# Attention with one projection per step in the transposes' banks, a score bank per head, and probabilities scaled on GpSimd

## The reference

```python
q = (h @ wq).reshape(b, s, 32, 64).transpose(0, 2, 1, 3)
k, v = ...                      # 8 heads, each repeated for 4 query heads
scores = jnp.einsum('bhqd,bhkd->bhqk', q, k) / jnp.sqrt(64.)
scores = jnp.where(causal, scores, jnp.finfo(scores.dtype).min)
attn = jax.nn.softmax(scores, axis=-1)
out = jnp.einsum('bhqk,bhkd->bhqd', attn, v)
h = x + out.reshape(b, s, 2048) @ wo
```

## Time and profile before

| | us |
|---|---|
| median of 3 runs | 2073.08 (2064.65 to 2074.55) |
| the profiled execution | 2076.18 |
| its span | 2074.5 |
| TensorE matmuls busy | 1878.1 (91%) |
| VectorE busy | 1062.9 (51%) |
| ScalarE busy | 899.0 (43%) |
| GpSimd busy | 234.4 (11%) |

### The profile page before, as it was taken

The page is one execution under the profiler, slowest core; times in us unless marked ns, Lnnn a source line. Parts: engine busy times, 40 slices in busy tenths (PEclk is TensorE's granted clock), DMA queues, the critical chain, the costliest instruction groups (busy, mean ns, idle before and its releaser), DMA issues.

```text
span 2074.5 us, 32988 instructions
## 1 busy us (share of the span) xinstructions
PE 1878.1 (91%) x12734; PEld 1440.2 (69%) x12734; DVE 1062.9 (51%) x1977; ACT 899.0 (43%) x2028; POOL 234.4 (11%) x369
## 2 busy tenths in 40 slices
PE   6999699999999999999999999999934999999970
PEld 5666366766766766766766767767734999999970
DVE  4666466666666666666666666666630111111116
ACT  3444255555555555555555555555530122212210
POOL 2222100000000000000000000000023000000014
PEclk9999799999999999999999999999966999999995
DMA  2000210000000000000000000000025042012503
GB/s 77 0 0 0 100 41 8 1 1 8 1 1 9 1 1 9 1 1 9 1 1 9 1 1 1 1 1 1 1 89 188 26 144 83 25 53 67 196 30 109
DMA packets 44296, 67.25 MB, mean 32 GB/s; under 512 B 9952, under 2 KB 34528, under 8 KB 44192
## 3 DMA queue, kind: packets, MB, share of 16 engines
q1 hardware_dynamic: 35920, 45.11, 6.6%
q0 software_dynamic: 6208, 18.62, 2.7%
q10 hardware_dynamic: 2064, 2.10, 0.3%
HBM read 140.52 MB, written 16.52 MB: 76 GB/s over the span
## 4 chain that ended last, share of the span: by engine, by line
PE 71%; DVE 13%; ACT 7%; issue 5%; POOL 1%; DMA 1%; SPq 1%; DVEq 0%; another core or an unknown queue 0%; POOLq 0%; ACTq 0%
PE wide L1288 13%; PE bank L1208 13%; PE bank L1196 10%; PE wide L1176 7%; PE bank L1297 7%; PE wide L1180 6%; PE bank L1217 3%; ACT qhl L578 3%; DVE qhl L813 3%; PE wide L1152 3%; ACT arena L584 2%; DVE nmax L820 2%; PE wide L1026 2%; PE bank L1015 2%; PE wide L1179 1%
## 5 line engine op out<-in xcount | busy, mean ns | idle before, releaser
L820 DVE TENSOR_REDUCE nmax<-wide 128x1 f32<-128x896 f32 (+7 forms) x512 | 386.6, 755 | 217.5 <-PE wide L1180 207.2
L584 ACT ACTIVATE arena<-wide,nmax 128x896 f32<-128x896 f32 (+7 forms) x512 | 380.6, 744 | 265.4 <-DVE nmax L820 260.4
L1176 PE MATMUL wide<-khi,qhl 128*128 128x512 f32 (+3 forms) x768 | 351.7, 458 | 28.5 <-DVE vt L804 25.1
L1196 PE MATMUL bank<-ident,arena 128*128 128x128 f32 x2304 | 308.5, 273 | 0.0
L592 ACT COPY arena<-bank 128x512 f32<-128x512 f32 (+1 forms) x352 | 192.8, 548 | 253.4 <-PE bank L1196 241.5
L1180 PE MATMUL wide<-klo,qhl 128*128 128x512 f32 (+3 forms) x768 | 300.6, 396 | 0.0
L1208 PE MATMUL bank<-arena,vt 128*64 128x256 f32 x2304 | 295.2, 403 | 0.0
L1288 PEld LDWEIGHTS wide<-wo,arena 128*128 128x128 f32 x2496 | 287.1, 193 | 3.2 <-issue 1.3
L1288 PE MATMUL wide<-wo,arena 128*128 128x128 f32 x2496 | 287.5, 276 | 0.9 <-ACT wo L638 0.9
L1196 PEld LDWEIGHTS bank<-ident,arena 128*128 128x128 f32 x2304 | 261.8, 140 | 8.7 <-issue 0.4
L950 DVE TENSOR_TENSOR wo<-wide,wo 128x512 f32<-128x512 f32 x78 | 54.0, 692 | 415.1 <-PE wide L1288 415.1
(11 more groups left out here) (194 smaller groups left out, 1867.6 us busy)
## 6 DMA issues: line engine op xcount, KB each, us to landing
arena<-in_L_ffn_w SPq DMA_DIRECT2D x117, 1024.0 KB
wo<-xs SPq DMA_DIRECT2D x40, 128.0 KB, 2.0
xs<-zeros POOLq DMA_DIRECT2D x1, 4992.0 KB, 20.6
ys<-y_sb POOLq DMA_DIRECT2D x39, 128.0 KB, 2.0
x_all<-in_L_attn_x ACTq DMA_DIRECT2D x1, 2048.0 KB, 9.9
wq_g<-in_L_ffn_wq SPq DMA_DIRECT2D x8, 256.0 KB, 2.9
wo<-in_L_ffn_wo SPq DMA_DIRECT2D x16, 128.0 KB, 8.0
out<-x_all SPq DMA_DIRECT2D x16, 128.0 KB
```

The costliest lines, as they stand in the source:

```text
L584: nc.scalar.activation(probs[t % 2][:, h, 0:w], score_bank(h)[:, 0:w], ACT.Exp, bias=nmax[:, t % 2, h:h + 1], accum_out=rsum[:, t % 2, h:h ...
L820: nc.vector.tensor_reduce(nmax[:, t % 2, h:h + 1], score_bank(h)[:, 0:w], AX.X, ALU.max, negate=True).then_inc(S("nmax_ready"), 1)
L1176: mm(dst, q, khi[:, lo:lo + cols], start=True, stop=False)
L1196: ins = nc.tensor.transpose(turned[j % 3][:, h * P:(h + 1) * P], probs[t % 2][:, h, m * P:(m + 1) * P], ident[:])
```

## The change

- Each step projects at most one item, at its end (`STEP_ITEM`, in the order H0, H1, H2, V2, F0, F1, F2, V1), and the item takes its turn in the three banks of the transposes (`TURNS`, `bank_of`, `wait_bank`). The first half of V is projected a step before its sequence.
- In tiles 0 to 3 of a sequence each head's scores have a bank of their own. In tiles 4 to 7 the pairs stay. The waits of score(t, h) follow from it (`scores_read`), and the fifth tile doesn't wait for items.
- The reciprocals are no longer spread or transposed. VectorE inverts the sums of two heads at a time (`invert`). GpSimd multiplies the probabilities in place, one head at a time (`normalise`): heads 0 and 1 in the step of the tile, heads 2 and 3 in the next. A tile's first transpose waits for all four.
- The product into `oT` becomes a copy on ScalarE, after exponent(t, 0).

```diff
-PLACES = {(0, "a"): "V1", (0, "b"): "H0", (1, "a"): "H1", (1, "b"): "H2", (2, "a"): "F0", (2, "b"): "F1", (3, "a"): "F2", (3, "b"): "V2"}
...
+STEP_ITEM = ["H0", "H1", "H2", "V2", "F0", "F1", "F2", "V1"]
...
+    kind, i = STEP_ITEM[ct]
+    if kind == "H":
+        item = n, int(i), 1
+    elif kind == "F":
+        item = n + 1, int(i), 0
+    else:
+        item = n + (i == "1"), "V", int(i) - 1
+    return item if item[0] < NSEQ else None
...
-    return n * (PAIRS + TB) + ct * (ct + 1) // 2 + ct
+    return n * PAIRS + ct * (ct + 1) // 2
...
-    blocks = t % TB + 2
+    blocks = t % TB + 1
     return range(blocks * p // 3, blocks * (p + 1) // 3)
+FIRST_ITEMS = [(0, 0, 0), (0, 1, 0), (0, 2, 0), (0, "V", 0)]
+TURNS = FIRST_ITEMS + [x for t in range(TILES + 1)
+                       for x in ([(t - 1, m) for p in range(3) for m in third(t - 1, p)] if t else []) + ([item_of(t)] if t < TILES and item_of(t) else [])]
+TURN_OF = {x: i for i, x in enumerate(TURNS)}
...
-            return wide[:, 1 + 2 * (ITEMS.index(item) % 2), :]
...
+        def score_bank(t, h):
+            if t % TB < TB // 2:
+                return wide[:, h, :]
             return wide[:, 2 * (h % 2):2 * (h % 2) + 2, :].rearrange("p a b -> p (a b)")
...
-        turned = [bank[0], bank[1], bank[3]]
+        shared = [bank[0], bank[1], bank[3]]
+        def bank_of(what):
+            return shared[TURN_OF[what] % 3][:]
...
+            def normalise(t, h):
+                w = (t % TB + 1) * P
+                gp.wait_ge(S("rinv_ready"), 2 * t + 1 + h // 2)
+                nc.gpsimd.tensor_scalar(probs[t % 2][:, h, 0:w], probs[t % 2][:, h, 0:w], rinv[:, t % 2, h:h + 1], None, ALU.mult).then_inc(S("probs_ready"), 1)
             for t in range(TILES + 1):
-                late, item = item_at(t - 1, "b") if t else None, item_at(t, "a")
-                if late and late[1] == 0:
-                    if t > 1:
-                        gp.wait_ge(S("rinv_spread"), t - 1)
-                    double(late[0], late[2])
-                    doubled += 1
                 if t:
-                    gp.wait_ge(S("k_doubled"), doubled)
-                    gp.wait_ge(S("rinv_ready"), t)
-                    nc.gpsimd.tensor_copy(spread[(t - 1) % 2].rearrange("p x (u d) -> p x u d", u=2),
-                                          rinv[:, (t - 1) % 2].rearrange("p (u x o) -> p x u o", x=2, o=1).to_broadcast([P, 2, 2, DH])).then_inc(S("rinv_spread"), 1)
+                    for h in (2, 3):
+                        normalise(t - 1, h)
+                item = item_of(t - 1) if t else None
                 if item and item[1] == 0:
-                    gp.wait_ge(S("rinv_spread"), t)
+                    gp.wait_ge(S("probs_ready"), G * t)
                     double(item[0], item[2])
                     doubled += 1
+                if t < TILES:
+                    gp.wait_ge(S("k_doubled"), doubled)
+                    for h in (0, 1):
+                        normalise(t, h)
...
             for t in range(TILES + 2):
-                if t and item_at(t - 1, "b"):
-                    evacuate(item_at(t - 1, "b"))
+                scored, turning, weighing = t < TILES, 1 <= t <= TILES, t >= 2
+                if t and t <= TILES and item_of(t - 1):
+                    evacuate(item_of(t - 1))
                 if scored:
                     exponent(t, 0)
+                if weighing:
+                    act.wait_ge(S("o2_psum"), t - 1)
+                    nc.scalar.copy(oT[:], bank[2][:, 0:2 * P].rearrange("p (j c) -> p j c", j=2)).then_inc(S("oT_ready"), 1)
...
+            def invert(t, pair_):
+                v.wait_ge(S("exp_done"), G * t + 2 * pair_ + 2)
+                hs = slice(2 * pair_, 2 * pair_ + 2)
+                nc.vector.reciprocal(rinv[:, t % 2, hs], rsum[:, t % 2, hs]).then_inc(S("rinv_ready"), 1)
+            for item in FIRST_ITEMS:
+                low_part(item)
             for t in range(TILES + 2):
                 scored, turning, weighing = t < TILES, 1 <= t <= TILES, t >= 2
-                late = item_at(t - 1, "b") if t else None
-                if late and late[1] == "V":
-                    low_part(late)
+                item = item_of(t - 1) if turning else None
                 if scored:
                     maximum(t, 0)
-                if late and late[1] != "V":
-                    low_part(late)
+                if item:
+                    low_part(item)
                 if turning:
-                    v.wait_ge(S("exp_done"), G * t)
-                    nc.vector.reciprocal(rinv[:, (t - 1) % 2], rsum[:, (t - 1) % 2]).then_inc(S("rinv_ready"), 1)
-                if weighing:
-                    v.wait_ge(S("o2_psum"), t - 1)
-                    v.wait_ge(*evacuated(blocks_before(t - 1) - 1))
-                    nc.vector.tensor_tensor(oT[:], bank[2][:, 0:2 * P].rearrange("p (j c) -> p j c", j=2), rbc[t % 2], ALU.mult).then_inc(S("oT_ready"), 1)
+                    invert(t - 1, 1)
                 if scored:
                     maximum(t, 1)
                 if turning:
                     evacuate_part(t - 1, 0)
                 if scored:
                     maximum(t, 2)
-                if item_at(t, "a"):
-                    low_part(item_at(t, "a"))
+                    invert(t, 0)
...
+            def wait_bank(what):
+                if TURN_OF[what] >= 3:
+                    before = TURNS[TURN_OF[what] - 3]
+                    if len(before) == 3:
+                        wait_taken(before)
+                    else:
+                        pe.wait_ge(*evacuated(blocks_before(before[0]) + before[1]))
             def project(item):
                 n, i, half = item
-                before = ITEMS.index(item) - 2
-                if before >= 0:
-                    wait_taken(ITEMS[before])
-                to = item_bank(item)
+                wait_bank(item)
+                to = bank_of(item)
...
+            def scores_read(t, h):
+                ct = t % TB
+                if ct == 0:
+                    return G * (t - 1) + 3 + h // 2
+                if ct < TB // 2:
+                    return G * (t - 1) + h + 1
+                if ct == TB // 2 and h < 2:
+                    return G * (t - 1) + 2 * h + 2
+                return G * t + h - 1
...
-                    for item in [x for x in ITEMS if x == (n, "V", 1) or x == (n + 1, 2, 0)]:
-                        wait_taken(item)
-                if c >= 2:
-                    pe.wait_ge(S("exp_done"), c - 1)
+                if t:
+                    pe.wait_ge(S("exp_done"), scores_read(t, h))
...
-                    j = blocks_before(t) + m
-                    if j >= 3:
-                        pe.wait_ge(*evacuated(j - 3))
+                    wait_bank((t, m))
+                    to = bank_of((t, m))
                     if m == 0:
-                        pe.wait_ge(S("exp_done"), G * (t + 1))
-                    if m == t % TB + 1:
-                        pe.wait_ge(S("rinv_spread"), t + 1)
-                        for x in range(2):
-                            ins = nc.tensor.transpose(turned[j % 3][:, x * P:(x + 1) * P], spread[t % 2][:, x], ident[:])
-                    else:
-                        for h in range(G):
-                            ins = nc.tensor.transpose(turned[j % 3][:, h * P:(h + 1) * P], probs[t % 2][:, h, m * P:(m + 1) * P], ident[:])
+                        pe.wait_ge(S("probs_ready"), G * (t + 1))
+                    for h in range(G):
+                        ins = nc.tensor.transpose(to[:, h * P:(h + 1) * P], probs[t % 2][:, h, m * P:(m + 1) * P], ident[:])
                     ins.then_inc(S("pT_psum"), 1)
...
-                if item_at(t, "a"):
-                    project(item_at(t, "a"))
...
-                if item_at(t, "b"):
-                    project(item_at(t, "b"))
+                if scored and item_of(t):
+                    project(item_of(t))
```

More of the change, by code:

```diff
@@ L43, with item_of @@
 TILES = NSEQ * TB
-PLACES = {(0, "a"): "V1", (0, "b"): "H0", (1, "a"): "H1", (1, "b"): "H2", (2, "a"): "F0", (2, "b"): "F1", (3, "a"): "F2", (3, "b"): "V2"}
-def item_at(t, place):
+STEP_ITEM = ["H0", "H1", "H2", "V2", "F0", "F1", "F2", "V1"]
+def item_of(t):
     n, ct = divmod(t, TB)
-    name = PLACES.get((ct, place))
-    if n >= NSEQ or name is None or (name[0] == "F" and n + 1 == NSEQ):
-        return None
-    if name[0] == "V":
-        return n, "V", int(name[1]) - 1
-    return (n, int(name[1]), 1) if name[0] == "H" else (n + 1, int(name[1]), 0)
-ITEMS = [(0, i, 0) for i in range(3)] + [x for t in range(TILES) for x in (item_at(t, "a"), item_at(t, "b")) if x]
+    kind, i = STEP_ITEM[ct]
[6 more added lines that the diff above has]
+    return item if item[0] < NSEQ else None
 def blocks_before(t):
     n, ct = divmod(t, TB)
-    return n * (PAIRS + TB) + ct * (ct + 1) // 2 + ct
+    return n * PAIRS + ct * (ct + 1) // 2
 def third(t, p):
-    blocks = t % TB + 2
```

(39 more changed lines are left out.)

16 lines of the change are left out of this document (5 added, 11 removed).

## The result

| | before | after |
|---|---|---|
| median of the runs | 2073.6 us | 2567.9 us (2566.7 to 2569.9) |
| span of the profiled execution | 2074.5 us | 2567.3 us |
| attention loop, first scores to last sum | 1247.2 us | 1736.9 us |
| TensorE idle in it | 26.8 us | 374.0 us |
| mean granted clock in it | 0.98 | 0.89 |

A forecast was written before the change was run, and what follows sets the result against it. TensorE's queue bounds the kernel, busy 1216.75 of the attention loop's 1243 us. From 2076.2 us, 78 taken away, 179 of stalls and 95 of slow stretches added: 2272, forecast as 2270 us, own range 2220 to 2330, whole range 2165 to 2475.

The forecast's parts named there:

- the path: First transpose waits for maximum(t,0), low_part, invert(t-1,1), then two GpSimd products: stalls of 179 us, against 78 us taken away.
- T0: The end of score(t,0), head 0's scores, on TensorE, from which the prediction counted each tile's times.
- the price of one product: GpSimd's in-place scaling of 128 x 128n: 0.44 + 0.106n us, so two take 1.30 to 2.58 us.
- late without products: GpSimd's start against TensorE's arrival at the first transpose, plus 0.1 us semaphore: 1.11 us (tile 3) to -1.93 (tile 0).
- slow stretches: Granted clock falls to 0.50 behind TensorE idle times from about 1.6 us: 1.7 us each, 3.5 a sequence, 95 us.
- slope alone, 2.9 ns a column, would give about 2600 us: Under rival 1, GpSimd's product costing slope and no start: about 2600 us, chance 0.03.
- The steeper end of the range: Rival 1, GpSimd's product at 0.33 + 0.22n us: 282 us of stalls, seven slow stretches, 2467 us; chance 0.28.
- Rival 3: The clock holds because the rest of the step is dense, so the stalls alone count: 2174 us; chance 0.12.
- 28 us for the reciprocals' transposes: On TensorE, 256 transposes at L1193 go, at a pitch of 0.11 us each: 28 us saved.
- 25 us for the fifth tile's wait: TensorE's 15 waits on VectorE's copy of V go, 25 us; their slow stretches were another 25 us.
- The faster rival: Rival 4: GpSimd's products nearly free, one flat length; 2043 us at 0.2 us each; chance 0.04, about break-even 0.02.
- The signs: If right: TensorE waits at the transposes' line, near 180 us in some 110 waits, longest in tiles 2 and 3.

The follow-up runs named there:

- The copies of the run above: The changed kernel with a GpSimd copy of the probabilities onto themselves in place of each product, so the probabilities are never divided: 2143.1 us.
- the kernel without scaling: The changed kernel with no scaling by the reciprocals on any engine, the first transpose waiting for the exponents: 2006.8 us, 0.972 of before.
- the short products: The changed kernel with every GpSimd product on the first 128 columns alone, all waits and their order kept: 2155.6 us.
- the banks-only kernel: The changed kernel with reciprocals spread and transposed and the product into oT as before, only projection order and banks new: 2044.4 us, ratio 0.986.

## Why the prediction was wrong

**What bounds the kernel, and that the path would cost more than it saves: right.** The path from maximum(t,0) over low_part and invert to two products was there. In the tile shown, GpSimd started 2.84 us after T0 (2.74 forecast), and in the next, whose scores end at 880.04 + 0.48, after 2.98 (2.87 forecast):

```profile
880.04 0.48 PE L1193 MATMUL wide<-klo,qhl 128*128 128x512 f32 x1
...
883.50 5.03 POOL L437 TENSOR_SCALAR arena<-arena,rinv 128x896 f32<-128x896 f32 x2 [3.69 <-DVE rinv L833]
```

TensorE came to the first transpose 870.58 - 3.93 - 863.21 = 3.44 us after T0 (3.30 forecast).

**The step that failed is the price of one product**, "I take 0.44 + 0.106n: the start of the same operation and, since it also reads one tensor, the copies' slope". The start was right within 0.06 us at one block and the slope was wrong by a factor of three. The runs have 0.285 + 0.32n us: 0.61 at one block, 2.85 at eight. Put into the prediction's own sum, this alone repairs it:

| tile | late without products | two products | stall by the sum | stall in the sequence shown |
|---|---|---|---|---|
| 2 | 1.09 | 1.85 | 2.94 | 2.71 |
| 3 | 1.11 | 2.49 | 3.60 | 3.25 |
| 4 | -0.60 | 3.13 | 2.53 | 2.26 |
| 5 | -0.75 | 3.77 | 3.02 | 2.74 |
| 6 | -0.46 | 4.41 | 3.95 | 3.93 |
| 7 | -0.86 | 5.05 | 4.19 | 4.16 |
| 0 | -1.93 | 5.69 | 3.76 | 3.72 |

The sum is 24.0 us a sequence, 384 us, against 364.6 measured. With seven slow stretches a sequence, 190 us, it gives 2076 - 78 + 384 + 190 = 2572 us, and the profiled execution took 2568.9. The parts agree too: idle time was to rise by 359 us and rose by 347, busy time by 137 and rose by 143. The case was among the rivals, as "slope alone, 2.9 ns a column, would give about 2600 us", with a chance of 0.03 and beyond the range (2.9 is 552 ns less the copies' start of 0.19 us, over 128 columns). That was too little for a price whose only row of the right kind was one instruction at one width: one width says nothing of the slope, and the slope was borrowed from another operation. That product reads one tensor, and it still takes three times as long per column as a copy and half as long again as a product of two tensors. The argument "it reads one tensor" had no row behind it. The steeper end of the range was set by the two-tensor product, on the same unfounded belief that it must be the dearer one.

**The rule for one-input work.** The prediction weighed the Trainium skill, GPSIMD Engine Reference, section "Engine selection": one-input elementwise work at roughly line rate. The copies of the run above agree (1.05 us at 1024 columns), the product with a scalar per partition does not (2.85 us), and the measurement decides. The opening of that page of the Trainium skill, that GpSimd is the wrong choice for ordinary elementwise arithmetic, held here: VectorE's product of 1024 columns took 0.75 us beside GpSimd's products of two tensors.

**The slow stretches.** Their sum came out right where stalls are long, in part by luck. 1737 us x (1 - 0.89) = 191 us at the clock's measure, as against TensorE's busy time 193.6 us above that of the kernel without scaling (1362.9 and 1169.4), in which the restarts after 113 stalls are too. But the 191 us are not seven equal stretches a sequence: tile 4's stall of 2.26 us brought none in 15 of 16 sequences, and tile 2's as a rule one of double length, in part beside idle time. Two more things were wrong. The 15 that went with the fifth tile's wait were worth 14 us and not 25. And an idle time of 1.6 to 1.7 us brings one in some sequences alone (9 of 32 stalls with the copies). With the short products, tile 2's stall of 2.06 us brought one in 7 of 16 sequences, and tile 3's of 1.97 us in all 16. Rival 3, the clock holding, was wrong for most long stalls and mostly right for the shortest.

**What was taken away.** 28 us for the reciprocals' transposes: 28 by the ratios, 34 by the loops, 37 by TensorE's busy time. 25 us for the fifth tile's wait: it is gone. With the output projection's new wait (4.7 us) the idle time of the banks-only kernel fell by 17.6 us, and in the changed kernel V's new wait for a bank takes 9.1 us. That V's projection waits for VectorE's evacuation of the block three turns earlier was not in the sum. The copy on ScalarE cost nothing, as said: 0.5 us in one wait.

**The faster rival.** It needed flat products of 0.3 to 0.4 us. The run with products of 0.60 us for every width took 2155.6 us, so its point of decision is not contradicted, and its condition was not near. By the prediction's own figures the 4.9 us a sequence are reached at 0.45 us if the clock holds, and at about 0.25 if the stalls of tiles 2 and 3 bring slow stretches.

**Smaller slips.** The rivals' totals start from 2073 us and the forecast's from 2076.2. Tile 0's 719.75 for GpSimd's start has no working behind it, 0.05 us from the row's 719.70. The signs were 113 waits, as said, but longest in tiles 6, 7 and 0 and not in 2 and 3, since the products grow with the tile.

What stays open is why the chip answers the same idle time with a slow stretch in one place and not in another. The length of the stall and the work around it do not settle it alone, since both are the same from sequence to sequence in the kernels with copies and with short products, where the answer changes. No run here moves one stall in time and leaves the rest.

## What to carry over

A new producer on another engine, between a result and the bound engine, has to be costed as a path with its queue: everything ahead of it on each engine, and the work itself at the widths in question. Here the place of a 0.16 us inversion was worth 374 us, and the choice of two heads of four for the engine that is on the path, with the inversion ahead of the item's low part, turned a loss of 24% into a gain of 2.5%. When the price of an operation has a row at one width only, take the slope from the dearest operation in reach, and leave room above it: here the product of two tensors gave 0.22 us a block, and the runs showed 0.32.

## What the runs showed of the hardware

- GpSimd, float32, 128 partitions, per column above the start: copy 0.84 ns, product of two tensors 1.67 ns, product with a scalar per partition 2.50 ns. The same scaling is shorter by a third as a product with a broadcast tensor (1.89 against 2.85 us at 1024 columns), and the kernel with it took 2314.1 against 2567.9 us.
- VectorE's product with a scalar, from and to the on-chip memory, took 0.69 us for 896 columns, less than a maximum over 896 columns of scores (1.09 us).
- When both scale at the same time, VectorE's product of 1024 columns took 1.14 us with GpSimd on the scalar form and 0.75 us with it on the tensor form; GpSimd's scalar form went from 2.85 to 3.09 us.
- Idle times of 1.60 and 1.72 us on TensorE left the granted clock at 1.00 in 23 of 32 cases in one kernel, where 1.64 us (2.11 once) brought 1.2 GHz all 15 times in the profile of another; in the changed kernel 2.26 us left it at 1.00 in 15 of 16 cases.
